# Four-layer attention chain on one core: full layers in another order, order of pieces set anew, score matmuls merged, transposed probabilities in two-bank units

## What is computed

```
x = L0(x)   # attention over positions: q, k of 32 channels, v of 256; softmax over 1024 keys; gamma*out + x
x = L1(x)   # group norm, then attention with q, k, v of 256 channels, projection, + x
x = L2(x)   # per position: layer norm; causal attention, 8 heads of 32, one shared k and v; projection, + x;
            # layer norm; feed-forward (layer norm, w1, layer norm, gelu, w2), + the normed value
x = L3(x)   # as L1, with its own weights
```

## Time and profile before

| what | us |
|---|---|
| time, median of 3 runs | 1485.58 (1484.95 to 1488.01) |
| the profiled execution | 1486.03 |
| its span, first to last instruction | 1484.2 |
| PE busy in it | 1338.0 |
| DVE busy | 870.6 |
| ACT busy | 595.3 |

### The profile page before, as it was taken

One profiled execution on the slowest core, in us unless ns is written; L12 is line 12 of the kernel. 1 busy time (PEld: TensorE's weight loads), 2 busy tenths in 40 slices (PEclk: granted clock), 3 DMA queues, 4 the chain that ended last, 5 costly groups with the idle time before them and its releaser, 6 DMA issues.

```text
span 1484.2 us, 22513 instructions
## 1 busy us (share of the span) xinstructions
PE 1338.0 (90%) x9152; PEld 1067.9 (72%) x9152; DVE 870.6 (59%) x1854; ACT 595.3 (40%) x973; POOL 92.5 (6%) x134
## 2 busy tenths in 40 slices
PE   5889989999999899989997899988999899998498
PEld 5768766777778777767776777776678777765486
DVE  3634466776458567557456657727656667675442
ACT  3523334344355343435334534423544443444142
POOL 0000000000000000000000000000010001001000
PEclk9999989999999899999998999997999999999699
DMA  5000010000000200010000010010000100100000
GB/s 176 1 1 0 29 43 23 1 23 2 1 1 2 70 11 14 22 29 1 2 1 0 6 38 23 2 49 3 1 2 1 43 2 23 37 16 1 0 1 29
DMA packets 20613, 27.09 MB, mean 18 GB/s; under 512 B 3488, under 2 KB 14240, under 8 KB 20512
## 3 DMA queue, kind: packets, MB, share of 16 engines
q1 hardware_dynamic: 20512, 25.66, 6.2%
HBM read 8.61 MB, written 4.19 MB: 9 GB/s over the span
## 4 chain that ended last, share of the span: by engine, by line
PE 79%; DVE 9%; ACT 6%; issue 2%; DMA 1%; SPq 1%; POOL 0%; ACTq 0%; DVEq 0%
PE ring L679 27%; PE ring L732 22%; PE ring L978 9%; PE ring L946 5%; PE ring L959 5%; PE ring L723 4%; ACT probs L1036 2%; PE ring L760 1%; PE ring L881 1%; ACT probsT L1049 1%; ACT cprobs L1205 1%; PE ring L948 1%; PE ring L916 1%; DVE part_max L1565 1%; SPq L595 1%
## 5 line engine op out<-in xcount | busy, mean ns | idle before, releaser
L732 PE MATMUL ring<-probsT,vt 128*128 128x256 f32 x1536 | 358.5, 387 | 16.7 <-ACT probsT L1049 16.4
L732 PEld LDWEIGHTS ring<-probsT,vt 128*128 128x128 f32 x1536 | 288.6, 193 | 67.4 <-ACT probsT L1049 20.6
L1205 ACT ACTIVATE cprobs<-ring 128x1024 f32<-128x1024 f32 (+1 forms) x160 | 150.4, 942 | 247.6 <-PE ring L959 246.9
L1036 ACT ACTIVATE probs<-ring,neg_max 128x1024 f32<-128x1024 f32 x96 | 107.1, 1116 | 185.4 <-DVE neg_max L1282 87.7
L1565 DVE TENSOR_REDUCE part_max<-ring 128x2 f32<-128x1024 f32 (+2 forms) x112 | 127.2, 1143 | 47.6 <-PE ring L946 34.2
L946 PE MATMUL ring<-ks,qs 96*128 96x512 f32 (+3 forms) x384 | 129.8, 421 | 16.4 <-ACT cprobs L1205 3.7
L1049 ACT COPY probsT<-ring 128x512 f32<-128x512 f32 x192 | 102.3, 592 | 48.2 <-PE ring L723 48.2
L959 PE MATMUL ring<-qs,ks 98*128 98x256 f32 (+1 forms) x640 | 114.5, 302 | 5.8 <-ACT probs L1036 1.4
L1281 DVE TENSOR_REDUCE shift_max<-ring 128x1 f32<-128x1024 f32 x64 | 78.3, 1224 | 70.3 <-PE ring L679 68.4
L723 PE MATMUL ring<-consts,probs 128*128 128x128 f32 x768 | 106.7, 279 | 13.1 <-ACT probs L1036 7.3
L959 PEld LDWEIGHTS ring<-qs,ks 98*128 98x128 f32 x640 | 91.4, 192 | 27.4 <-issue 15.6
(11 more groups left out here) (215 smaller groups left out, 2212.1 us busy)
## 6 DMA issues: line engine op xcount, KB each, us to landing
x<-x_dram SPq DMA_DIRECT2D x4, 1024.0 KB, 6.5
qs<-q_hi SPq DMA_DIRECT2D x32, 128.0 KB, 2.3
qs<-q_hi SPq DMA_DIRECT2D x64, 64.0 KB, 2.0
out_dram<-z SPq DMA_DIRECT2D x6, 512.0 KB, 2.8
qs<-q_lo SPq DMA_DIRECT2D x16, 128.0 KB, 2.3
qs<-max_rows SPq DMA_DIRECT2D x128, 2.0 KB
qs<-q_lo SPq DMA_DIRECT2D x32, 64.0 KB, 2.0
out_dram<-x SPq DMA_DIRECT2D x2, 512.0 KB, 2.8
```

The costliest lines, as they stand in the source:

```text
L732: last = mm(o[:, ct * QUARTER:(ct + 1) * QUARTER], vt[:, j, ct * P:(ct + 1) * P], probsT[:, qi % (NQ - 1), j, :], start=j == 0, stop=j == ...
L1036: A(probs[:, ti % 2, :], flat(full_name(l, b, ("s", ti))), ACT.Exp, bias=neg_max[:, ti:ti + 1], accum_out=row_sum[:, ti:ti + 1]).then_inc( ...
L1205: A(causal_probs(step, n), heads(name)[:, :, 0:n], ACT.Exp).then_inc(read_done["c", "act"], 1)
```

## The change

- `FULL`: `L1.3` comes before `L3.1`, where it came after.
- `ORDER`: all five strings are new. Before, the last 58 causal pieces on TensorE (from `C3.exp` of block 6 on) stand in a row without a full piece, and `L3.3` follows. Now the pieces of `L3.2` stand between them up to the end of `C3`.
- `causal_exponents`: in one bank the heads are one matmul. Four matmuls of 256 columns become two of 512 (128 pieces), four of 128 become one of 512 (32 pieces).
- `causal_max`: first the score matmuls of all heads of a piece, then their masks; before, they alternated.
- `full_turn`, `turned`: eight transposes into one unit of two banks, and one copy of 1024 columns in the place of two of 512.
- `home`: `L3.1` lies in `x[1]`, element 3 in `z` from L0 on. The wait of `w2` for stores goes. In its place SP loads element 3 only after both stores of `L3.0` have landed. The group-norm statistics of L3 get two buffers.

```diff
-FULL = [("L0", 0), ("L1", 0), ("L0", 1), ("L1", 1), ("L0", 2), ("L3", 0), ("L1", 2), ("L0", 3), ("L3", 1), ("L1", 3),
+FULL = [("L0", 0), ("L1", 0), ("L0", 1), ("L1", 1), ("L0", 2), ("L3", 0), ("L1", 2), ("L0", 3), ("L1", 3), ("L3", 1),
         ("L3", 2), ("L3", 3)]
...
-        "ha5cFaCFgdaCgCFcaCegcaCecahecaCcegaCCbCdCfCgaCcCegahCcCheCaChCCChfCgahabC72F406F2F4062F450F672F450FFF6F541F3"
+        "ga4cgFa2FeaCe2a4haCC2e0CcFC4hC2hFa4C0cFCeh26aFfCcCFaFeC1dFC5aC3CFCc5h1FFCCaF3F510hFbFF3fg7FCFF01F350F2F4602F4"
...
-    out += turn(0) + [("s", 3)] + turn(1) + [("s", 4)] + turn(2) + [("o", 0), ("s", 5)] + turn(3)
-    out += [("s", 6)] + turn(4) + [("o", 1), ("s", 7)] + turn(5)
-    return out + turn(6) + [("o", 2)] + turn(7) + [("o", 3)]
-def turn(ti):
-    return [("t", 2 * ti), ("t", 2 * ti + 1)]
+    out += [("t", 0), ("s", 3), ("t", 1), ("s", 4), ("t", 2), ("o", 0), ("s", 5), ("t", 3), ("s", 6), ("t", 4), ("o", 1)]
+    return out + [("s", 7), ("t", 5), ("t", 6), ("o", 2), ("t", 7), ("o", 3)]
...
         def home(l, b):
-            return x[b % 2] if l != "L3" else x[0] if b == B - 1 else z
+            return (z, x[1], x[0], z)[b] if l == "L3" else (x[0], x[1], x[0], z)[b]
...
             def full_chain():
-                for b in range(2, B):
-                    wait_filled(sp, f"C{b - 2}.xt1")
-                    sp.dma_start(home("L0", b)[:, :, :], x_dram[b]).then_inc(x_in[b % 2], 16)
-                    yield
-                for b in range(B):
+                wait_filled(sp, "C0.xt1")
+                sp.dma_start(home("L0", 2)[:, :, :], x_dram[2]).then_inc(x_in[0], 16)
+                yield
+                yield from stores(0)
+                sp.wait_ge(y_out, 16 * NB)
+                sp.dma_start(home("L0", 3)[:, :, :], x_dram[3]).then_inc(x_in[1], 16)
+                yield
+                for b in range(1, B):
                     yield from stores(b)
...
-            def full_turn(l, b, n, i):
-                ti, hf = divmod(i, NB)
-                o = open_unit(full_name(l, b, ("t", i))).rearrange("p b (s n) -> p (b s) n", n=P)
+            def full_turn(l, b, n, ti):
+                o = open_unit(full_name(l, b, ("t", ti))).rearrange("p b (s n) -> p (b s) n", n=P)
                 pe.wait_ge(probs_scaled[SCALED_BY[n]], scaled_no(n, ti))
-                for j in range(TPH):
-                    last = nc.tensor.transpose(o[:, j, :], probs[:, ti % 2, (TPH * hf + j) * P:(TPH * hf + j + 1) * P],
-                                               ident)
+                for j in range(NT):
+                    last = nc.tensor.transpose(o[:, j, :], probs[:, ti % 2, j * P:(j + 1) * P], ident)
                 last.then_inc(filled["f"], 1)
...
                 elif kind == "w2":
-                    if 0 < b < B - 1 and hf == 0:
-                        pe.wait_ge(y_out, 16 * NB * b)
...
-                for i in range(4) if two == 2 else range(2):
-                    o = heads(name)[:, i, 0:hi - lo] if two == 2 else slot(name)[:, i, 0:hi - lo]
+                own = 4 // width[name] if two == 2 else 1
+                outs = [(heads(name) if two == 2 else slot(name))[:, i, 0:hi - lo] for i in range(4 if two == 2 else 2)]
+                for i, o in enumerate(outs):
                     a = i if two == 2 else 2 * two + i
-                    last = mm(o, stack(k, a, 3 * DH, at, at + P), ks[0:3 * DH, lo:hi], start=True, stop=not diag)
-                    if diag:
-                        last = mm(o[:, hi - lo - P:hi - lo], mask[:, 0, :], mask[:, 1, :], start=False, stop=True)
+                    last = mm(o, stack(k, a, 3 * DH, at, at + P), ks[0:3 * DH, lo:hi], start=i % own == 0,
+                              stop=not diag and i % own == own - 1)
+                if diag:
+                    for i, o in enumerate(outs):
+                        last = mm(o[:, hi - lo - P:hi - lo], mask[:, 0, :], mask[:, 1, :], start=False,
+                                  stop=i % own == own - 1)
...
-                for a in range(4):
-                    last = mm(heads(name)[:, a, 0:n], ks[0:3 * DH + 2, jt * P:(jt + 1) * P],
-                              stack(k, a, 3 * DH + 2, QUARTER - n, QUARTER), start=True, stop=True)
+                own = 4 // width[name]
+                for a in range(0, 4, own):
+                    last = mm(heads(name)[:, a:a + own, 0:n], ks[0:3 * DH + 2, jt * P:(jt + 1) * P],
+                              stack(k, slice(a, a + own), 3 * DH + 2, QUARTER - n, QUARTER), start=True, stop=True)
...
             def turned(l, b, ti):
-                for i in range(2 * ti, 2 * ti + 2):
-                    name = full_name(l, b, ("t", i))
-                    js = slice(TPH * (i % 2), TPH * (i % 2 + 1))
-                    wait_filled(act, name)
-                    nc.scalar.copy(probsT[:, ti // 2 % (NQ - 1), js, (ti % 2) * P:(ti % 2 + 1) * P],
-                                   slot(name)[:, 0, :].rearrange("p (s n) -> p s n", n=P)
-                                   ).then_inc(read_done["f", "act"], 1)
-                    yield
+                name = full_name(l, b, ("t", ti))
+                wait_filled(act, name)
+                nc.scalar.copy(probsT[:, ti // 2 % (NQ - 1), :, (ti % 2) * P:(ti % 2 + 1) * P],
+                               slot(name).rearrange("p b (s n) -> p (b s) n", n=P)).then_inc(read_done["f", "act"], 1)
```

87 lines of the change are left out of this document (45 added, 42 removed).

## The result

| | us (median, lowest to highest) | to before, 95% interval |
|---|---|---|
| before | 1485.26 (1484.59 to 1488.01) | 1 |
| changed | 1432.53 (1432.07 to 1433.88) | 0.9643 [0.9626, 0.966] |

The median before, 1485.26, has one run more than the table ahead of the change, which gives 1485.58. The change saves 52.7 us, 3.6%. The forecast was 1445, so 41 us; the direction and the range were right, and the gain came out 12 us larger. The profiled execution of the changed kernel took 1432.07 us.

What follows compares the result with a forecast made beforehand. PE bounds the kernel (busy 1338 of 1484 us, 79% of the chain). Terms -20 - 4 - 6 - 12 + 3 - 2 = -41 us gave 1445 us, 2.7% less; range 1420 to 1472.

Steps and rivals of the forecast that it cites:

- The end of C3, holes (-20): Last 80 us before L3.3: L3.2 pieces between the lone pieces cut PE idle time from 24.2 to 4.3 us.
- One sign: In the new profile, no stretch near the end has over 12% of PE idle time.
- The end of C1 (-6): Around C1's end, now beside L1.2 and not L0.3, PE idle time falls by 6 us (0 to 12).
- The clock (-4): At the end of C3, less work at 1.2 GHz saves 4 us (0 to 6).
- The gain is at most 6 us: Cap on the clock gain at C3's end: up to 8.2 us lost at half speed before, 1.8 after.
- Merged exponents (-8) and masks (-7), less a fifth: -12: On PE, merged exponent scores save 8 us and masks behind scores 7; 79% of these 15 counts, 12 us.
- Two-bank transposes (+3): A tile's last column comes 420 ns later at 16 PE waits before value pieces: costs 3 us (0 to 7).
- Buffers (-2): The two waits of `w2` for stores, 3.3 us, go: saves 2 us (0 to 3); element 3's load stays hidden.
- better order everywhere: Second rival: the new order beats the old everywhere, interleaved idle share 5% not 7.1%: 1419 us; chance 12%.
- Holes that move: First rival: holes move instead of closing, as ACT and DVE also run in fixed order: 1462 to 1480 us; chance 17%.
- PSUM as the bound: Third rival: two-bank tiles make PE wait at unit openings, 49 us, 1494 in all; above 1489 us, chance 7%.
- no change: Fourth rival: the old holes were DVE's slack, so all gains come back, within 0.2%; chance 3%.

Runs made afterwards that it cites:

- order alone: Changed kernel with new order and buffers but the old instructions (alternating masks, four exponent matmuls, one-bank transposes): 1437.44 us.
- C3 alone: Changed kernel with L3.2's pieces first in the last stage, then the last 50 causal pieces of C3 in a row, then L3.3: 1472.63 us.
- exchanged layers: Kernel before with L1.3 and L3.1 exchanged and the new buffers, old instructions, old strings but SP's: 1486.0 us.
- merged: Kernel before, old order, buffers and one-bank transposes, with exponent scores merged and masks behind all scores: 1479.14 us.
- one bank: Changed kernel with transposes in two one-bank units at the same places and two ACT copies of 512 columns: 1424.99 us.

## Why the prediction was right, and where its sizes were off

**What bounds the kernel.** Right. PE has 82% of the chain of the changed kernel, and DVE and ACT kept 870 to 872 and 588 to 596 us of work in every kernel while the time moved by 70 us.

**The end of C3, holes (-20).** Right: 4.3 us of idle time were forecast for the work that stood alone, and the window of 80 us has 4.3 (the window doesn't hold quite the same pieces, so the exact match is luck; the whole stage of C3, with 57 us more of work in it, gave 15.4 and not 20). The longest wait for a layer norm there was forecast under 3 us and is 0.74. One sign was set too tight: L3.3 alone is idle for 13% of its stretch, over the 12% named, but it was so before as well.

**The end of C1 (-6).** Right in place, low in size: 12.6 us of idle time became 3.5, inside the bounds of 0 to -12. The row of C2's end was taken as its measure. C2's own end became worse, 6.1 to 8.6, so the row of one end didn't measure another. By stage, C1 gave 10.8 and C3 15.4 us; all holes together, with the order alone, 34.7 where the terms made 28.

**The clock (-4).** This is the term that was mis-sized most. The prediction counted only the lone 80 us, and of them only what the work in them could lose. The order alone made the same instructions 15.3 us shorter. The clock rose outside the end of C3 too: around the end of C1 from 0.91 to 1.00. The step that failed is "The gain is at most 6 us". It held the clock for a matter of one stretch, while the other stages of before were not at full clock either: 0.96 in those of C1 and C2, and 0.97 over the interleaved part. In the medians the order brought 16 us more than its terms, in the two spans 18: 11 of these lie here and 7 in the holes. The two-bank units took 4.5 of it back.

**Merged exponents (-8) and masks (-7), less a fifth: -12.** In the new order the merges took 1437.44 - 1424.99 = 12.4 us, as forecast. Their PE time is 1322.7 - 1306.2 = 16.5 us, of which the clock (0.972 to 0.974, 80 to 74 us at 1.2 GHz) is some 2, so 14 stand against the 15 of the forecast; PE's idle time grew by 3.4 us. That the sum fits is partly luck: the exponents came out at 6.4 us for the 8 forecast, the masks at 9 for the 7. In the old order the same edit brought 6 to 7 us, since its clock fell to 0.952. The 79% were a fair factor for the new order (12.4 of 14) and too much for the old one. That is shown; why the clock fell there is not.

**Two-bank transposes (+3).** The sign was right and the size was less than half: 7.5 us. The bound of 7 stood on 16 waits with 0.42 us each. The waits for copies grew by 4.0 us, within it: the short ones by some 0.37 each, those of 2 us not. Two things were left out. With one bank a unit the first copy can run beside the second four transposes, and a unit of two banks needs both free before its first transpose. In the spans, 9.3 us apart, 5.3 are idle time and 4.0 are work; the clock (0.974 against 0.971) accounts for some 3 of those 4. The banks' being held is 0 to 3 us of the 7.5, their being opened together up to 1.4. The rule on banks in the Trainium skill, "Perfetto Trace Analysis", section "Matmuls", points the right way: work on one bank should overlap the emptying of another. The runs tell which half of it counts here: the overlap, more than the bank's being free. ACT's saving was put at 16.5 us and is 4.5 (595.3 to 590.8). The reading of the earlier trace rows was at fault: 192 copies with a mean of 592 ns keep ACT busy for 102.3 us and not 113.7, since two in a row overlap. It lies beside PE in any case.

**Buffers (-2).** The waits of `w2` for stores are gone from the list of PE's waits. On its own that brought nothing (1486.0). The load of element 3 landed in time: the x loads took 7.5 us (6.5 before), and no wait of PE for them appears.

**The sum.** By measured parts: the order 47.8, the merges 12.4, the two banks -7.5, together 52.7. They are the steps of one chain of kernels from before to the changed one, so they must add up, and the sum confirms nothing; another order of the steps gives other sizes (54.2 for the order with merged instructions, 6 to 7 for the merges in the old order). The rival "better order everywhere" (1419) was half true in its time and not in its mechanism: the idle share of the interleaved part fell only from 7.1 to 6.8%, not to 5%, and the clock gave much of what the holes didn't. Holes that move, PSUM as the bound and no change didn't happen. PE's busy time near 1320 came out at 1310: the clock's 15.3 in the place of 4 are the difference. The range's share left out was given as 2 in 10, where its own parts make 24.5%.

## What to carry to other kernels

A stretch in which TensorE, the bounding engine, stands alone on a serial path costs its holes, and here about half as much again by its clock (13.6 us beside 29.1, 15.3 beside 34.7). So estimate the clock over the whole span and not only in the stretch: in these kernels each microsecond less at 1.2 GHz was worth a third of a microsecond of work. Before making the units larger that one engine hands to another, ask when the first part of a unit can move: here two small copies, the first beside the transposes of the second, and values that start on the half that is there, brought 17 us, while the larger unit had saved ACT 4.5 us of work that nobody waited for. Merging matmuls paid where they were short (four of 128 columns into one: 0.16 us) and hardly where they were longer (four of 256 into two: 0.01 us).

## What the runs showed of the hardware

- Work against clock. In four pairs of kernels with the same matmuls in another order, PE's busy time and the time at 1.2 GHz (from the mean clock) differ by 15.3 and 45 us (before, order alone), 13.6 and 41 (changed, C3 alone), 6.1 and 18 (before, exchanged layers) and 23.8 and 68 (merged, one bank). That is 0.33 to 0.35 us of work for each us, with mean clocks of three digits, so that each of the four times at 1.2 GHz is good to some 3 us. Work that ran throughout at 1.2 in the place of 2.4 GHz would give 0.5; why it is less isn't shown.
- Two kernels with the same layers at the same place, before and merged, kept 55.77 us of busy time in the lone 80 us of C3 at clocks of 0.83 and 0.80. So the sum of the holes and of the work doesn't fix how much of a stretch is at the lower clock. What else sets it stays open.
- Masks (128 columns, 128 bf16 weights) follow each other every 0.05 us. Putting them behind their scores saved 0.22 us for a group of four scores of 256 columns, and 0.07 us for four of 128, two of 384 or two of 512.
- One ACT copy of 1024 columns from PSUM takes 1008 ns, two of 512 take 590 each; but of two in a row the busy time is 101.7 us for 192, 0.53 each. So a pair takes 1.06 us, 0.05 more than the one copy and not the 0.17 that the means suggest.
